# Denominators copied one key tile sooner, their reciprocal behind the first unit's statistics, and the next pair's scales ahead of the last unit's

## The chip, the core and the metric

The kernel runs on one core of a Trainium2 chip. The metric is device time in microseconds (us), the median of several executions; lower is better. Beside the executions that were timed there is one that the hardware profiler recorded.

## What is computed

Two layers over x of shape (8, 768, 32, 32), in float32; each adds its result to its input.

```python
N = H * W                                              # 1024 tokens, 12 heads of 64
x_flat = swapaxes(gn(x).reshape(B, C, N), 1, 2)
q, k, v = split(x_flat @ W_qkv.T)                      # q is not used further
var_v, var_k = var(v, ddof=1), var(k, ddof=1)          # over the 64 channels of a head
scores = var_v @ swapaxes(var_k) * hd ** -0.5          # an outer product, N x N for each head
out = softmax(scores) @ v
x = x + from_tokens(out @ W_proj.T + b_proj)           # layer 0
# layer 1: each channel group of gn(x) is shifted by a whole offset, masked and
# smoothed with a 3 x 3 kernel made of the offset's rest
x = x + displace(gn(x), offset)
```

gn normalises over groups of 24 channels. The scores of a head have rank one, so one row of exponentials is exp(scale of the key x row of the queries).

## The kernel before

Batches follow each other; in a loop over them, the attention of batch b + 1 (function `span`) runs beside the displacement (layer 1) of batch b. Batch 0 is handled ahead of the loop and has no layer-1 work beside it. Every engine has its own program, in which the order is written out by hand; they meet at semaphores alone.

**A batch.** A phase A makes the first six units of K and V (`kv_unit`: two tiles of 128 tokens for one pair of heads, 72 matmuls, line 1096); four units make a pair. Then come six pairs of heads, p = 0 to 5 (MT = 8 key tiles of 128 each, m = 0 to 7). Behind them the output is projected (`phase_c`, line 1150).

**A pair on TensorE.** Two units of a later pair, the weighting of V by the exponentials for key tiles 0 to 3 (`weigh`, line 1135), the two transposes of `k_transpose` (lines 1105, 1106), two more units, the small matmul of `k_spread` (line 1110), key tiles 4 to 7, and the denominators (line 1117) at the end. In pair 4 only two units are left, the transposes stand behind key tile 1 and the spread behind key tile 3; pair 5 has none of these. TensorE's queue stands at the transposes until VectorE has made `kmx` (line 770).

**On ScalarE.** `exps` makes the two exponentials of a key tile (line 607) into a ring of eight; they need the pair's scales `coef` and the broadcast row `a_sb`. `d_copy` copies the denominators of the pair before out of PSUM (line 614). `middle_tap` belongs to layer 1 (line 631), `v_evict` takes V out of PSUM once the unit's statistics are done (line 591).

**On VectorE.** `add_up` adds the exponentials of tiles 1 to 6 (in pairs 4 and 5: 1 to 4) into a sum for each head (line 805); the second head's sum of tile 1 waits for the denominators of the pair before (semaphore `s_d`). `kv_stats` takes the statistics of a unit out of PSUM (line 754), `variances` makes kmx of them, `k_max` (lines 777 to 780) and `k_scales` (lines 785, 788) the scales of the next pair. `d_reciprocal` (line 809) inverts the denominators, `o_normalise` (line 816) uses them; the rest is layer 1's: `taps_y` and `gn` at m = 3, `taps_x` (lines 859 to 864) at m = 6.

**The denominators' way.** They are copied on ScalarE into `d_sb`, spread over 128 partitions by four small DMAs of SyncE (`dt_sb`, line 407), inverted on VectorE, written to DRAM (line 411), broadcast to `r_t` (line 420) and multiplied in at m = 4. The scales' way goes through SyncE too: `at`, to DRAM (line 392), broadcast to `a_sb` (line 401). SyncE works its queue in order. GpSimd writes layer 1's rows to DRAM and gathers the shifted windows from there (line 498).

In code, the waits that the prediction comes to:

```python
act.wait_ge(s_d, b * NP + p + 1)                  # d_copy: denominators complete
dve.wait_ge(s_dt, (b * NP + p) * 64 + 64)         # d_reciprocal: the four DMAs have landed
pe.wait_ge(s_kmx, b * NP + q + 1)                 # k_transpose
dve.wait_ge(s_kmp, b * NP + q + 1)                # k_scales: the spread matmul is done
```

Of the kernel before, what the change touches and what calls it, by code (L numbers as in the profile page):

```python
# [38 lines left out]
def gn_attention_displace(nc, x, w_qkv, w_proj, b_proj, offset, out):  # L39
# [44 lines left out]
    with ctx:  # L84
# [478 lines left out]
        def _(act):  # L563
# [29 lines left out]
            def exps(b, p, m):  # L593
                for s in (0, 1):
                    h = 2 * p + s
                    i = (p * MT + m) * 2 + s
                    if m == 0:
                        if s == 0:
                            act.wait_ge(s_coef, b * NP + p + 1)
                        act.wait_ge(s_a[h % 4], a_count(b, h))  # L600
                    if i >= RING:

                        pj, mj = divmod((i - RING) // 2, MT)
                        act.wait_ge(s_pv, b * (NT // 2) + (i - RING) // 2 + 1)
                        if mj < MD[pj]:
                            act.wait_ge(s_acc, b * NADD + add_count(pj, s, mj))
                    nc.scalar.activation(ring_of(p, s, m), a_sb[:, h % 4, :], ACT.Exp,  # L607
                                         scale=coef[:, h, m:m + 1]).then_inc(s_exp, 1)

            def d_copy(b, p, later):  # L610
                act.wait_ge(s_d, b * NP + p + 1)
                if later or p:
                    act.wait_ge(s_dt, (b * NP + p) * 64)
                nc.scalar.activation(d_sb[:, :], ps[:, D_BANK, :], ACT.Copy).then_inc(s_dsb, 1)
# [11 lines left out]
            def middle_tap(b, t):  # L626

                act.wait_ge(s_sh, (b * CT + t + 1) * 16)
                if t:
                    act.wait_ge(s_fin, b * CT + t)  # L630
                nc.scalar.activation(t_t, g_t, ACT.Copy, scale=taps[:, t, 1, 1:2]).then_inc(s_tap, 1)
# [7 lines left out]
            def span(b, l1, with_next, beside=None):  # L639
                later = l1 is not None  # L640
                for p in range(NP):
                    nxt = UA + p * UQ
                    for m in range(MT):
                        if not later and p == 0 and m == 3:
                            act.wait_ge(s_pads, 2 * CT * 16)
                        exps(b, p, m)
                        if p and m == (3 if p <= 4 else 2):
                            d_copy(b, p - 1, later)
                        if m == 3:
                            if later:  # L650
                                middle_tap(l1, p)
                            if p <= 4:
                                v_evict(b, nxt)
                                v_evict(b, nxt + 1)
                        if m == 7:
                            if p:
                                o_first(b, p - 1)
                            if 1 <= p <= 4:
                                add_bias(b, p - 1)
                            if p <= 3:  # L660
                                v_evict(b, nxt + 2)
                                v_evict(b, nxt + 3)
                        if with_next and (p, m) in X_LOADS:
                            load_x(b + 1, X_LOADS[p, m])
                        if beside is not None:
                            beside(p, m)
# [59 lines left out]
        def _(dve):  # L726
# [20 lines left out]
            def kv_stats(b, u):  # L747

                q, g = divmod(u, UQ)
                dve.wait_ge(s_kv, b * NU + u + 1)  # L750
                for m in (0, 1):
                    for c in range(4):
                        lo = m * 2 * P + c * HD
                        ins = nc.vector.bn_stats(st[:, 2 * g + m, c, :], ps[:, kv_bank[u % 2], lo:lo + HD])  # L754
                ins.then_inc(s_bn, 1)
# [26 lines left out]
            def k_scales(b, q):  # L782

                dve.wait_ge(s_kmp, b * NP + q + 1)
                nc.vector.tensor_tensor(coef[:, 2 * q:2 * q + 2, :], m2[:, 2:4, :],
                                        ps_km.unsqueeze(2).broadcast_to((P, 2, MT)), ALU.subtract).then_inc(s_cch, 1)
                dve.wait_ge(s_cch, b * NP + q + 1)
                nc.vector.tensor_scalar(coef[:, 2 * q:2 * q + 2, :], coef[:, 2 * q:2 * q + 2, :], var_f8[:, 0:1], 0.0,
                                        ALU.mult, ALU.min).then_inc(s_coef, 1)
# [97 lines left out]
            def span(b, l1, with_next, beside=None):  # L887
                later = l1 is not None
                for p in range(NP):
                    nxt = UA + p * UQ  # L890
                    for m in range(MT):
                        add_up(b, p, m, later)
                        if m == 2:
                            if p:
                                d_reciprocal(b, p - 1)
                            if p <= 4:
                                kv_stats(b, nxt)
                        if m == 3:
                            if p <= 4:
                                kv_stats(b, nxt + 1)  # L900
                                variances(b, p + 1)
                            if p == 4:
                                k_max(b, p + 1, later)
                            if later:
                                taps_y(l1, p, g_t, t_t)
                                if p + 1 < CT:
                                    gn(l1, p + 1, g_t)
                        if m == 4:
                            if p <= 3:
                                k_max(b, p + 1, later)  # L910
                            if p == 4:
                                k_scales(b, p + 1)
                            if p:
                                o_normalise(b, p - 1)
                        if m == 5 and p <= 3:
                            kv_stats(b, nxt + 2)
                        if m == 6:
                            if p <= 3:
                                kv_stats(b, nxt + 3)
                                k_scales(b, p + 1)  # L920
                            if later:
                                taps_x(l1, p, t_t)
                        if m == 7 and p:
                            if p == NP - 1 and with_next:
                                x_stats(b + 1, (0, 1))
                            o_second(b, p - 1)
                        if beside is not None:
                            beside(p, m)
# [331 lines left out]
```

## Time and profile before

| | |
|---|---|
| median of 3 runs | 2263.07 us (2258.71 to 2267.14) |
| the profiled execution's own time | 2257.91 us |
| its span, first to last instruction | 2256.3 us |
| mean granted clock of TensorE | 0.956 of full speed |
| TensorE busy | 2036.6 us, 90% |
| VectorE busy | 1676.5 us, 74% |
| ScalarE busy | 1179.1 us, 52% |
| GpSimd busy | 192.3 us, 9% |

The profiled execution lies 5.2 us under the median; what surrounds its span is 1.6 us. The shares are means over stages: a phase A, the pairs and the group's end have different limits. PE stands for TensorE, PEld for its loads of weights, DVE for VectorE, ACT for ScalarE, POOL for GpSimd and SP for SyncE; a q behind a name marks what its sequencer does, such as issuing a DMA.

### The profile page before, as it was taken

The numbers are of one execution on the slowest core, as the hardware profiler recorded it, in microseconds if no ns is written. First come the engines' busy times: TensorE is split into PE (matmuls) and PEld (weight loads), VectorE is DVE, ScalarE is ACT, GpSimd is POOL, SyncE is SP. The second block draws the span as 40 slices with busy tenths as digits, with TensorE's granted clock in tenths as the row PEclk, the third lists the DMA queues.
The fourth block names the chain that finished last, engine by engine and source line by source line (L and its number), as shares of the span: only waits on it lengthen the run. The fifth ranks groups of instructions, "written<-read, shape, count | busy, mean of one in ns | idle before, by whom it ended". The sixth has DMA issues, their size and how long they took to land.

```text
span 2256.3 us, 36312 instructions
## 1 busy us (share of the span) xinstructions
PE 2036.6 (90%) x13036; PEld 1118.5 (50%) x13036; DVE 1676.5 (74%) x3695; ACT 1179.1 (52%) x1285; POOL 192.3 (9%) x215
## 2 busy tenths in 40 slices
PE   3899999998999999999899989999899999999970
PEld 2665346552655436563375625655265543665330
DVE  7676566986678865887668976698668886688837
ACT  5466525664266742667336752566426674265701
POOL 2000000110001100110000100011000110011001
PEclk7999999999999999999999999999999999999995
DMA  6311302334023521335113350233412342133304
GB/s 241 132 49 58 95 11 95 114 115 131 11 100 118 160 68 39 104 110 173 30 53 118 114 161 11 95 114 120 126 31 84 120 163 57 39 119 118 104 20 168
DMA packets 106989, 219.14 MB, mean 97 GB/s; under 512 B 53024, under 2 KB 53792, under 8 KB 106784
## 3 DMA queue, kind: packets, MB, share of 16 engines
q1 hardware_dynamic: 74816, 100.12, 15.1%
q0 software_dynamic: 25920, 94.38, 11.4%
q10 hardware_dynamic: 6048, 22.02, 2.9%
q8 instruction: 114, 1.87, 0.3%
q14 instruction: 91, 0.75, 0.1%
HBM read 158.28 MB, written 57.80 MB: 96 GB/s over the span
## 4 chain that ended last, share of the span: by engine, by line
PE 37%; DVE 27%; DMA 13%; ACT 10%; issue 8%; SPq 3%; POOL 1%; DVEq 0%; ACTq 0%; POOLq 0%
PE ps L1150 13%; PE ps L1135 12%; DVE bt L805 10%; PE ps L1096 9%; ACT ring L607 8%; DVE st L754 6%; DMA a_sb<-a_rows 3%; DMA dt_sb<-d_sb 3%; PE ps L1117 3%; SPq L407 3%; DMA bt<-r_rows 2%; DMA a_rows<-at 2%; DVE bt L849 2%; DVE bt L846 1%; DVE bst_x L728 1%
## 5 line engine op out<-in xcount | busy, mean ns | idle before, releaser
L607 ACT ACTIVATE ring<-a_sb,coef 128x1024 f32<-128x1024 f32 x768 | 810.7, 1136 | 48.5 <-DMA a_sb<-a_rows 33.1
L1096 PE MATMUL ps<-wkv_hi,h_sp 128*128 128x256 f16 x4608 | 786.8, 276 | 11.8 <-DVE h_sp L745 9.9
L1135 PE MATMUL ps<-ring,xv 128*64 128x512 f32 x3072 | 704.0, 606 | 1.4
L1096 PE MATMUL ps<-wkv_lo,h_sp 128*128 128x256 f16 x2304 | 634.7, 275 | 0.0
L1096 PEld LDWEIGHTS ps<-wkv_hi,h_sp 128*128 128x128 f16 x4608 | 455.5, 99 | 103.4 <-issue 31.8
L805 DVE TENSOR_TENSOR bt<-bt,ring 128x1024 f32<-128x1024 f32 x416 | 487.7, 1212 | 1.4 <-ACT ring L607 1.4
L1135 PEld LDWEIGHTS ps<-ring,xv 128*64 128x64 f32 x3072 | 210.0, 139 | 421.3 <-issue 386.5
L591 ACT ACTIVATE xv<-ps 128x256 f32<-128x256 f32 x192 | 73.5, 383 | 653.2 <-DVE st L754 653.2
L1150 PE MATMUL ps<-xv,wp_hi 128*128 128x512 f16 x1152 | 358.9, 389 | 41.0 <-DVE xv L820 28.3
L754 DVE BATCH_NORM_STATS2 st<-ps 128x6 f32<-128x64 f32 x1536 | 216.5, 209 | 57.8 <-PE ps L1096 56.9
L1096 PEld LDWEIGHTS ps<-wkv_lo,h_sp 128*128 128x128 f16 x2304 | 227.8, 99 | 28.1
L1150 PE MATMUL ps<-xv,wp_lo 128*128 128x512 f16 x576 | 224.5, 390 | 0.0
L1150 PEld LDWEIGHTS ps<-xv,wp_hi 128*128 128x128 f16 x1152 | 115.2, 100 | 205.0 <-issue 46.8
L805 DVE TENSOR_TENSOR bt<-ring 128x1024 f32<-128x1024 f32 x96 | 114.3, 1221 | 99.7 <-ACT ring L607 76.6
L809 DVE RECIPROCAL dt_sb<-dt_sb 128x16 f32<-128x16 f32 x48 | 12.1, 253 | 174.4 <-DMA dt_sb<-d_sb 174.4
L624 ACT ACTIVATE xv<-bt 128x1024 f16<-128x1024 f32 x48 | 50.6, 1055 | 160.5 <-DVE bt L816 159.2
L949 DVE SCALAR_TENSOR_TENSOR xv<-ps,proj_f,xv 128x512 f32<-128x512 f32 x96 | 71.3, 745 | 68.9 <-PE ps L1150 68.6
L816 DVE TENSOR_TENSOR bt<-ps,bt 128x1024 f32<-128x1024 f32 x48 | 58.2, 1213 | 73.9 <-DMA bt<-r_rows 73.9
L498 POOL DMA_INDIRECT bt<-shift_rows,first_i x42 | 83.4, 1986 | 162.8 <-DMA shift_rows<-bt 117.1
L1150 PEld LDWEIGHTS ps<-xv,wp_lo 128*128 128x128 f16 x576 | 57.6, 100 | 67.5 <-issue 6.0
L1117 PE MATMUL ps<-ring,ones 128*32 128x512 f32 x640 | 85.2, 605 | 0.0
L506 POOL DMA_DIRECT2D shift_rows<-bt x42 | 23.3, 556 | 633.1 <-DVE bt L834 633.1
(122 smaller groups left out, 1341.3 us busy)
## 6 DMA issues: line engine op xcount, KB each, us to landing
a_sb<-a_rows SPq DMA_DIRECT2D x96, 512.0 KB, 4.8
xv<-in_x POOLq DMA_DIRECT2D x48, 512.0 KB, 3.7
bt<-r_rows SPq DMA_DIRECT2D x96, 256.0 KB, 3.9
h_sp<-in_x ACTq DMA_DIRECT2D x42, 512.0 KB, 4.1
shift_rows<-bt POOLq DMA_DIRECT2D x42, 512.0 KB, 2.9
out<-xv POOLq DMA_DIRECT2D x42, 512.0 KB, 2.9
shift_rows<-ring SPq DMA_DIRECT2D x12, 528.0 KB, 14.0
xv<-in_L_conv_W_qkv SPq DMA_DIRECT2D x4, 1152.0 KB, 8.9
```

The costliest lines, as they stand in the source:

```text
L407: sp.dma_start(dt_sb[32 * g:32 * g + 32, :], d_sb[32 * g:32 * g + 1, :]).then_inc(s_dt, 16)
L498: nc.gpsimd.indirect_dma_start(dst, None, shift_rows[t].rearrange("c r -> (c r)").unsqueeze(0), bass.IndirectOffsetOnAxis(first_i[:, t:t + ...
L591: nc.scalar.activation(v_sb[:, q, 2 * g:2 * g + 2, :], src[:, :, 0:P], ACT.Copy, scale=V_DOWN).then_inc(s_vev, 1)
L607: nc.scalar.activation(ring_of(p, s, m), a_sb[:, h % 4, :], ACT.Exp, scale=coef[:, h, m:m + 1]).then_inc(s_exp, 1)
L754: ins = nc.vector.bn_stats(st[:, 2 * g + m, c, :], ps[:, kv_bank[u % 2], lo:lo + HD])
L805: nc.vector.tensor_tensor(acc_of(p, s), one, ring_of(p, s, m), ALU.add).then_inc(s_acc, 1)
L816: nc.vector.tensor_tensor(r2, ps[:, k:k + 2, :], r2, ALU.mult).then_inc(s_on, 1)
L949: nc.vector.scalar_tensor_tensor(cut, ps[:, pj_bank[u % 6], :], proj_f[:, 0:1], cut, ALU.mult, ALU.add).then_inc(s_x1, 1)
L1096: last = nc.tensor.matmul(ps[:, kv_bank[u % 2], half * 2 * P:(half + 1) * 2 * P], h_sp[:, k, hp, m * P:(m + 1) * P], wkv[wpart][:, k, q * ...
L1117: last = nc.tensor.matmul(ps[32 * g:32 * g + 32, D_BANK, :], ones[:, 0:32], tiles[s][:, j * HALF:(j + 1) * HALF], start=start, stop=stop)
L1135: last = nc.tensor.matmul(ps[s * HD:(s + 1) * HD, o_bank[p % 2] + j, :], v_sb[:, p, m, s * HD:(s + 1) * HD], ring_of(p, s, m)[:, j * HALF: ...
L1150: last = nc.tensor.matmul(ps[:, pj_bank[u % 6], :], wp[wpart][:, k, t * P:(t + 1) * P], o_sp[:, k, op, j * HALF:(j + 1) * HALF], start=(k ...
```

## The change

In each pair, `d_copy` stands behind the exponentials of key tile 2 on ScalarE; so far it stood behind those of tile 3 in pairs 1 to 4, and behind tile 2 in pair 5. On VectorE, `d_reciprocal` moves from key tile 2 to key tile 3, and the statistics of the pair's first unit, which stood behind the reciprocal, move there too and stand ahead of it. The sums of tile 3 thereby come ahead of both. In pairs 0 to 3, `k_scales` stands ahead of the statistics of the last unit.

```diff
@@ ScalarE, span
                         exps(b, p, m)
-                        if p and m == (3 if p <= 4 else 2):
+                        if p and m == 2:
                             d_copy(b, p - 1, later)
@@ VectorE, span
                         add_up(b, p, m, later)
-                        if m == 2:
+                        if m == 3:
+                            if p <= 4:
+                                kv_stats(b, nxt)
                             if p:
                                 d_reciprocal(b, p - 1)
-                            if p <= 4:
-                                kv_stats(b, nxt)
-                        if m == 3:
                             if p <= 4:
                                 kv_stats(b, nxt + 1)
                                 variances(b, p + 1)
...
                         if m == 6:
                             if p <= 3:
+                                k_scales(b, p + 1)
                                 kv_stats(b, nxt + 3)
-                                k_scales(b, p + 1)
                             if later:
                                 taps_x(l1, p, t_t)
```

## Rows read from the trace of the kernel before

**Rows 1.** The page's first part: busy time, share of the span, instructions.
```profile
PE 2036.6 (90%) x13036; PEld 1118.5 (50%) x13036; DVE 1676.5 (74%) x3695; ACT 1179.1 (52%) x1285; POOL 192.3 (9%) x215
```

**Rows 2.** Totals of waits: who waited for whom, us, times, the longest.
```profile
DVE dt_sb L809 <- DMA dt_sb<-d_sb: 174.4, 48, 10.0
...
PE ps L1105 <- DVE kmx L770: 58.7, 30, 4.2
...
ACT ring L607 <- DMA a_sb<-a_rows: 33.1, 18, 3.7
```

**Rows 3.** Busy time by stretch: pairs 1 to 4 of batch 0; batches 1 to 7 summed.
```profile
128.52:252.47 123.95, 123.95 (x859) 69.89 (x860) 88.19 (x235) 80.05 (x89) 0.00 (x0) 1.00 0.24 70
...
sum 921.39, PE 882.48 PEld 491.63 DVE 785.44 ACT 623.59 POOL 114.01; mean PE 126.07 PEld 70.23 DVE 112.21 ACT 89.08 POOL 16.29
```

**Rows 4.** The same view, batch 4: pairs 1, 2, 4, and behind a wait.
```profile
core 0: us, PE busy (x) PEld busy (x) DVE busy (x) ACT busy (x) POOL busy (x), PEclk, DMA share, GB/s
...
1192.43:1224.77 32.34, 32.34 (x230) 19.20 (x230) 27.14 (x63) 20.84 (x24) 3.83 (x3) 1.00 0.35 116
1224.77:1257.84 33.07, 32.41 (x230) 19.19 (x230) 29.46 (x65) 21.96 (x25) 4.37 (x4) 1.00 0.35 113
...
1290.88:1323.54 32.66, 28.51 (x175) 12.53 (x176) 26.22 (x47) 24.67 (x26) 4.04 (x5) 0.95 0.55 170
...
1306.50:1308.00 1.50, 1.42 (x4) 0.39 (x6) 0.72 (x5) 1.25 (x2) 0.00 (x0) 0.50 0.88 208
```

**Rows 5.** TensorE in time: start, length, [idle before, released by]; batch 0, then 4.
```profile
237.34 3.65 PE L1135 MATMUL ps<-ring,xv 128*64 128x512 f32 x16
...
1173.46 0.38 PE L1105 MATMUL ps<-ident,av 128*16 128x128 f32 x1 [2.98 <-DVE kmx L770]
...
1240.42 0.28 PE L1105 MATMUL ps<-ident,av 128*16 128x128 f32 x1 [0.66 <-DVE kmx L770]
...
1306.58 0.38 PE L1105 MATMUL ps<-ident,av 128*16 128x128 f32 x1 [4.15 <-DVE kmx L770]
...
1307.11 4.96 PE L1135 MATMUL ps<-ring,xv 128*64 128x512 f32 x16
```

**Rows 6.** VectorE in time, pair 4 of batch 4.
```profile
1292.89 2.35 DVE L805 TENSOR_TENSOR bt<-ring 128x1024 f32<-128x1024 f32 x2
1295.16 2.35 DVE L805 TENSOR_TENSOR bt<-bt,ring 128x1024 f32<-128x1024 f32 x2
1300.90 0.25 DVE L809 RECIPROCAL dt_sb<-dt_sb 128x16 f32<-128x16 f32 x1 [3.39 <-DMA dt_sb<-d_sb]
...
1304.33 1.14 DVE L754 BATCH_NORM_STATS2 st<-ps 128x6 f32<-128x64 f32 x8
...
1306.37 0.16 DVE L770 TENSOR_REDUCE kmx<-m 128x2 f32<-128x16 f32 x1
```

**Rows 7.** ScalarE in time, pairs 4 and 5 of batch 4.
```profile
1288.34 8.43 ACT L607 ACTIVATE ring<-a_sb,coef 128x1024 f32<-128x1024 f32 x8 [0.18 <-issue]
1296.67 0.57 ACT L614 ACTIVATE d_sb<-ps 128x512 f32<-128x512 f32 x1
...
1324.19 2.18 ACT L607 ACTIVATE ring<-a_sb,coef 128x1024 f32<-128x1024 f32 x2
...
1326.27 1.14 ACT L631 ACTIVATE bt<-bt,taps 128x1024 f32<-128x1024 f32 x1
```

**Rows 8.** VectorE in time, pair 5 and the end of batch 4.
```profile
1329.67 0.25 DVE L809 RECIPROCAL dt_sb<-dt_sb 128x16 f32<-128x16 f32 x1 [2.48 <-DMA dt_sb<-d_sb]
...
1354.45 0.25 DVE L809 RECIPROCAL dt_sb<-dt_sb 128x16 f32<-128x16 f32 x1 [4.58 <-DMA dt_sb<-d_sb]
...
1365.77 1.22 DVE L816 TENSOR_TENSOR bt<-ps,bt 128x1024 f32<-128x1024 f32 x1 [8.02 <-DMA bt<-r_rows]
```

**Rows 9.** VectorE in time, pair 0 of batch 4, its first sums.
```profile
1163.33 2.36 DVE L805 TENSOR_TENSOR bt<-ring 128x1024 f32<-128x1024 f32 x2 [7.31 <-ACT ring L607]
```

**Rows 10.** GpSimd in time, pair 4 of batch 4: the gather of the last windows.
```profile
1319.33 1.85 POOL L498 DMA_INDIRECT bt<-shift_rows,first_i  x1 [6.52 <-DVE xv L864]
```

## The prediction

> **What bounds the kernel now.** I read the page first: TensorE is busy 2036.6 us of a span of 2256.3, twenty points ahead of VectorE's 1676.5 [rows 1], so a change is worth what it takes from TensorE's idle time and from the time that its matmuls run slowly. The totals of waits come next. TensorE's largest wait by name is that of its transpose (line 1105) for VectorE's maxima kmx: 58.7 us in 30 waits. VectorE's largest is that of the reciprocal (line 809) for the denominators' DMA: 174.4 us, all 48 times [rows 2]. Are they one chain? In pair 4 of batch 4 VectorE's order answers: two tiles of sums (each tile is two additions), 3.39 us of waiting for the DMA, reciprocal, then the statistics and sums on which kmx hangs, kmx finished at 1306.53, and 0.05 us later TensorE goes on, after 4.15 us [rows 5, 6]. So the DMA's lateness is passed on to TensorE.
>
> What a pair costs without such a wait is in the trace: batch 0 has no layer-1 work on VectorE, its transposes never wait, and TensorE is busy for all 123.95 us from the end of pair 0's denominators to the end of pair 4's. The same stretch in batches 1 to 7 takes 921.39 us together, TensorE 882.48 of them busy, with as many matmuls [rows 3]. The excess over 7 x 123.95 = 867.65 is 53.74 us: 921.39 - 882.48 = 38.9 idle, and 14.8 in which the same matmuls took longer. The second part is the clock. In pair 4, behind the 4.15 us wait, the granted clock is 0.50 of full speed (the lower of the two levels, 1.2 GHz), and 16 matmuls take 4.96 us that in batch 0 took 3.65 [rows 4, 5]. Behind the wait of 0.66 in pair 2 it stays at 1.00 [rows 4, 5]. By pairs in batch 4: pair 1 takes 32.34 and has nothing to lose, pair 2 takes 33.07 (0.7 too much, and pair 3 repeats it), pair 4 32.66 where 26.92 do (that is 123.95 less three times 32.34) [rows 3, 4], 5.74 too much.
>
> **The change, part by part.** It adds and removes no instruction; three are moved. I count from S, the end of the denominators' matmuls of the pair before: 1290.88 for pair 4 of batch 4 [rows 4].
>
> *The copy.* Eight exponentials take 8.43 us, and the copy (0.57) stands behind them at 1296.67 [rows 7]. Behind six it starts 8.43 x 2/8 = 2.1 us sooner, at 1294.6. What it reads is complete at S, so it needn't wait here. SyncE is idle until then, and the four small DMAs behind it start 2.1 sooner too. From the copy's end (1297.24) to the reciprocal (1300.90) is 3.66 us [rows 6, 7], so the data are there at 1298.8. Queued behind the copy are the exponentials of tile 3, 0.5 later: ready at 1297.3, when VectorE is still at tile 2's sums (until 1297.51) [rows 6]. Hidden, and ScalarE is busy 21.96 of 33.07 us in pair 2 [rows 4].
>
> *The reciprocal and the first statistics behind tile 3's sums.* VectorE's new order in pair 4: sums until 1297.5, tile 3's sums 2.27 more (as from 1292.89 to 1295.16) to 1299.8, first statistics 1.1 to 1300.9, reciprocal 0.2 to 1301.1 with its data there since 1298.8, second statistics and the small chain 2.2 (1304.33 to 1306.53) to 1303.3 [rows 6]. TensorE wants kmx at 1306.58 - 4.15 = 1302.43, S + 11.55. So with nothing else moved the wait falls from 4.15 to 0.9.
>
> *The same with the pairs before it gaining too.* VectorE starts pair 4's sums 2.0 us behind S [rows 6] because the pair before stalled it 3.3 as well; its work in pair 2 is 29.46 us where TensorE's pair is 32.34 at best [rows 4], so without the stalls it catches up within a pair or two. Then the sums begin at S + 0.2 at best (one of them waits for those denominators), end at S + 5.9 with tile 3's, and the first statistics end at S + 7.0. The copy, if ScalarE has run ahead, waits for S, and its data land at S + 0.7 + 3.66 = 4.4: no stall. The second statistics can't start before TensorE's second unit ends: S + 7.9 (1302.43 less 3.65 for the two key tiles between, 1298.8), and kmx is there at S + 10.2. Pairs 1 to 3 want it at S + 15.0 (1240.42 - 0.66 - 1224.77), pair 4 at S + 11.55 [rows 4, 5]. All four waits go, and with pair 4's its slow matmuls. I take the full 53.7; the other bound, 0.9 kept in each pair 4 and the clock up, is 53.7 - 6.3 = 47.4. For pair 5 and the end of the group I take nothing: the copy there was behind tile 2 already, and the reciprocal has its data only at 1329.67, after a wait of 2.48 [rows 8], into which tile 3's sums (2.27) now fall. That chain hangs on the pair's denominators, which shift as a whole.
>
> *Pair 0* keeps its wait. No reciprocal is in it; VectorE sits idle 7.31 us until the exponentials come and then works without a break to kmx, in either order [rows 9]. So some 2.98 us of waiting stay in a batch, with the slow clock behind them (that transpose took 0.38 where pair 2's took 0.28) [rows 5].
>
> *The scales ahead of the last statistics.* The coefficients come by one set of statistics sooner (1.14 long [rows 6]), the last unit's statistics later by two operations on 16 columns, some tenths of a us, and with them ScalarE's copy of V and the next exponentials. TensorE wants the first of these at S + 7.9 = 1298.8; they begin at 1288.34 [rows 7]. With ten us between, the price is nothing. If VectorE has run ahead it now waits for TensorE's spread matmul, which comes directly after that unit: another few tenths, inside its 2.9 of slack.
>
> *What is late next.* The projection and pair 5 follow TensorE. Pair 5's exponentials of tile 3 come 2.5 us ahead of need now (1326.37 [rows 7] against three key tiles behind the pair's start, 1323.54 + 3 x 1.8 = 1328.9 [rows 4, 5]). Walk ScalarE's queue through the new pair 4: tile 4's exponentials start at S + 9.6, when TensorE has freed the ring; four tiles, 8.4, S + 18.0; then it waits for VectorE's normalisation (kmx at 10.2, the answer from TensorE at some 12, layer 1's three operations 3.8, tile 4's sums 2.3, scales 0.4, normalisation 1.2: S + 20.4), two operations of 1.1, S + 22.6; six exponentials, the copy and two more, 9.0, S + 31.6. TensorE wants them at S + 26.9 + 5.4 = 32.3: a margin of 0.7. Thin, but on this side.
>
> The sum: 2257.91 - 53.7 = 2204.2 for an execution like the profiled one. The median of before is 2263.07, 5.2 above that one; the forecast for a median is 2263.07 - 53.7 = 2209.4, and I say 2210.
>
> **Rivals.**
> *Part of pair 4's wait stays* (VectorE doesn't catch up, pair 5 is held a little by ScalarE, or the clock falls by chance at another place). 0.9 kept in seven batches is 2216; with the slow matmuls too, which cost 5.74 - 4.15 = 1.6 in batch 4, 6.3 + 11 = 17 us, 2227. For it: the thin margin in pair 5. Against: VectorE's 2.9 us of slack.
> *GpSimd's gathers.* In pair 4 the gather of the windows stood 6.52 us until VectorE's operation at line 864 ended [rows 10]. A VectorE without idle gaps leaves fewer openings. The middle tap of pair 5, which stands ahead of tile 4's exponentials, waits for that gather (1319.33 to 1326.27, 6.94 us at most [rows 7, 10]). A gather that is pushed behind two more VectorE operations costs some 2 us in pair 5: 7 x 2 = 14, 2223. The Trainium skill speaks for this one (page "SBUF — State Buffer", section "Who interferes with whom"): VectorE with two SBUF inputs and a GpSimd instruction that reads SBUF exclude each other for whole instructions. [...]
> *No change:* exponentials too late. Everything up to kmx now hangs behind tile 3's exponentials and the copy. Were they as late as in pair 0, kmx would still be late. The loads of a_sb make them wait 33.1 us in all, 18 times [rows 2], mostly in pairs 0 and 1; it would have to be every pair. 2255 to 2263.
> *Slower:* the reciprocals' way back. In pairs 1 to 3 the normalisation stands in VectorE's queue at about S + 16.7 (kmx 10.2, layer 1's operations 3.8, tile 4's sums 2.3, the maxima 0.4), and the reciprocal ends at S + 7.1. Where VectorE waited for this way at the end of batch 4 it took 11.07 us (1354.70 to 1365.77, amid other loads) [rows 8]. Over 9.6 VectorE waits; over 9.6 + 2.9 of slack + 1.3 in pair 4 TensorE does. At 17.5 us it would lose some 3.7 in each of three pairs, 11 for the 7.7 gained: 2263 + 7 x 3.4 = 2287. It decides from about 16.5 us, half as long again as that.
>
> **How the numbers follow.** Full gain 0.66 (2200 to 2217: the runs of before spread by 4 either side, and the clock may fall in more or fewer of the seven pairs 0); part of pair 4's wait 0.14 and the gathers 0.12 (2215 to 2236); no change 0.04; slower 0.04. A difference under 0.5%, 11 us, is about what a measurement of this kernel can't tell from none. Faster 0.92, within 0.04, slower 0.04. Range 2198 to 2236: it leaves out the last two cases and the ends of the others.
>
> **What would show it.** Right: in pairs 1 to 4 no wait at line 1105, pair periods of 32.3 and pair 4 at 26.9, the clock at 1.00 through pair 4; VectorE's wait at line 809 gone in pairs 1 to 4, its idle time now at the first sums and before the second statistics; total wait at line 1105 about 20 us, all of pair 0. Wrong: waits of TensorE at line 1135 in pair 5, a wait at line 816 in pairs 1 to 4, or a pair 4 still at half clock.

## The result and the profile after

The changed kernel takes 2205.32 us (median of four runs, 2201.63 to 2210.82), the kernel before, on the same chip, 2261.9 (2258.71 to 2267.14). The ratio is 0.975, with a 95% interval of 0.9717 to 0.9782: faster by 2.5%, and 5 us below the forecast of 2210. The profiled execution has a time of 2210.82 and a span of 2209.2, the longest of its four, where the profiled one of before was the shortest of its own; so the two spans differ by 47.1 us and the medians by 56.6. Of the page, the engines' busy time first:

```profile
PE 2025.0 (92%) x13036; PEld 1118.1 (51%) x13036; DVE 1681.8 (76%) x3695; ACT 1183.2 (54%) x1285; POOL 190.5 (9%) x215
```

Against [rows 1] TensorE is busy 11.6 us less with the same 13,036 matmuls, because fewer of them run at the lower granted clock. Next the totals of waits of the changed kernel (who waited for whom, us, times, the longest). TensorE's transposes are one line higher now, at 1104.

```profile
DVE bt L816 <- DMA bt<-r_rows: 90.4, 16, 8.0
DVE bt L805 <- ACT ring L607: 85.4, 29, 7.7
...
DVE dt_sb L809 <- DMA dt_sb<-d_sb: 45.0, 21, 9.4
...
ACT ring L607 <- DMA a_sb<-a_rows: 40.0, 27, 3.8
...
DVE bt L805 <- PE ps L1116: 35.8, 26, 2.4
...
PE ps L1104 <- DVE kmx L770: 19.9, 7, 3.0
```

The wait for kmx has fallen from 58.7 us in 30 waits [rows 2] to 19.9 in seven, one for each pair 0; the reciprocal's from 174.4 in 48 to 45.0 in 21, those of pair 5 and of the groups' ends, and short ones of 0.3 to 1.0 in pair 1. Next the busy time by stretch: first pairs 1 to 4 together, of batches 1, 4 and 7, with the sum over batches 1 to 7; then pairs 1, 4 and 5 of batch 4 one by one.

```profile
core 0: us, PE busy (x) PEld busy (x) DVE busy (x) ACT busy (x) POOL busy (x), PEclk, DMA share, GB/s
388.93:512.87 123.94, 123.94 (x858) 69.96 (x860) 113.37 (x237) 88.77 (x97) 15.81 (x16) 1.00 0.40 131
...
1172.85:1296.80 123.95, 123.95 (x858) 69.92 (x860) 111.65 (x237) 86.72 (x95) 16.46 (x16) 1.00 0.38 127
...
1950.94:2074.88 123.94, 123.94 (x858) 69.92 (x860) 113.36 (x237) 88.60 (x96) 15.93 (x16) 1.00 0.36 123
sum 867.61, PE 867.61 PEld 489.52 DVE 788.12 ACT 614.16 POOL 111.66; mean PE 123.94 PEld 69.93 DVE 112.59 ACT 87.74 POOL 15.95
```

```profile
1172.85:1205.19 32.34, 32.34 (x229) 19.23 (x230) 30.26 (x65) 24.32 (x27) 4.38 (x4) 1.00 0.40 131
...
1269.87:1296.80 26.93, 26.93 (x175) 12.23 (x176) 21.97 (x44) 18.40 (x20) 3.31 (x4) 1.00 0.45 147
1296.80:1320.97 24.17, 23.79 (x120) 6.99 (x120) 19.23 (x20) 16.03 (x16) 1.07 (x2) 1.00 0.54 177
```

TensorE is now busy for the whole of each stretch, at a clock of 1.00: 867.6 us against the 921.39 of [rows 3], 53.8 less. VectorE does the same work (788.12 us, before 785.44 [rows 3]). The last row has something new, pair 5 at 24.17 us with a gap of 0.4 in it. Pair 4 of batch 4 in time, where S is 1269.87; TensorE first (with the transpose of pair 0), then VectorE, then ScalarE:

```profile
1153.75 0.28 PE L1104 MATMUL ps<-ident,av 128*16 128x128 f32 x1 [2.98 <-DVE kmx L770]
...
1281.36 0.28 PE L1104 MATMUL ps<-ident,av 128*16 128x128 f32 x1
1281.67 3.65 PE L1134 MATMUL ps<-ring,xv 128*64 128x512 f32 x16
...
1302.47 1.94 PE L1134 MATMUL ps<-ring,xv 128*64 128x512 f32 x8 [0.37 <-ACT ring L607]
```

```profile
1270.03 1.23 DVE L805 TENSOR_TENSOR bt<-ring 128x1024 f32<-128x1024 f32 x1 [1.46 <-PE ps L1116]
1271.17 4.62 DVE L805 TENSOR_TENSOR bt<-bt,ring 128x1024 f32<-128x1024 f32 x4
1275.71 1.15 DVE L754 BATCH_NORM_STATS2 st<-ps 128x6 f32<-128x64 f32 x8
1276.77 0.24 DVE L809 RECIPROCAL dt_sb<-dt_sb 128x16 f32<-128x16 f32 x1
1277.88 1.15 DVE L754 BATCH_NORM_STATS2 st<-ps 128x6 f32<-128x64 f32 x8 [0.87 <-PE ps L1095]
...
1279.93 0.16 DVE L770 TENSOR_REDUCE kmx<-m 128x2 f32<-128x16 f32 x1
```

```profile
1270.02 0.60 ACT L614 ACTIVATE d_sb<-ps 128x512 f32<-128x512 f32 x1 [0.68 <-PE ps L1116]
...
1292.85 1.15 ACT L607 ACTIVATE ring<-a_sb,coef 128x1024 f32<-128x1024 f32 x1 [0.73 <-DMA a_sb<-a_rows]
1294.55 1.15 ACT L607 ACTIVATE ring<-a_sb,coef 128x1024 f32<-128x1024 f32 x1 [0.55 <-DMA a_sb<-a_rows]
```

The transpose waited 4.15 us at this place and the 16 matmuls behind it took 4.96 [rows 5]; now it doesn't wait and they take 3.65. VectorE waits for TensorE twice (1.46 and 0.87 us), which means that it has caught up; the reciprocal finds its data there.

To see what each change moved I compare stages. A stage runs from one end of the denominators' matmuls of a pair to another, in the profiled execution; "between" is from pair 5's end to the end of the next pair 0, seven times (us).

| kernel | median | ratio [95%] | pairs 1-4, batches 1-7 | pair 5, all 8 | between |
|---|---|---|---|---|---|
| before | 2261.9 | | 921.4 | 188.6 | 783.5 |
| after | 2205.32 | 0.975 [0.9717, 0.9782] | 867.6 | 190.3 | 786.1 |
| copy alone | 2234.88 | 0.9882 [0.9839, 0.9924] | 897.9 | 188.6 | 782.7 |
| order alone | 2206.11 | 0.9739 [0.9695, 0.9783] | 867.6 | 189.9 | 784.6 |
| scales alone | 2265.19 | 1.0015 [0.9995, 1.0034] | 925.1 | 188.6 | 784.7 |
| later transposes | 2252.77 | 0.9962 [0.9941, 0.9984] | 911.5 | 196.1 | 780.2 |
| after, again | 2207.45 | 0.9762 [0.9735, 0.9789] | 867.6 | 191.2 | 789.0 |
| after + pair 0 | 2179.98 | 0.9645 [0.9617, 0.9673] | 867.6 | 191.4 | 757.5 |
| copy later | 2292.17 | 1.0145 [1.0109, 1.018] | 957.4 | 188.6 | 780.6 |
| copy behind tile 1 | 2204.59 | 0.9727 [0.971, 0.9745] | 868.3 | 189.1 | 784.5 |
| copy alone, small x load | 2201.39 | 0.9713 [0.9684, 0.9741] | 867.6 | 188.6 | 781.4 |
| before, small x load | 2252.42 | 0.9935 [0.9915, 0.9955] | 917.8 | 188.6 | 780.0 |
| pair 0 + x loads | 2181.76 | 0.9637 [0.9613, 0.9661] | 867.6 | 188.6 | 764.5 |
| pair 0, order only | 2180.62 | 0.9631 [0.9607, 0.9655] | 867.6 | 190.3 | 758.9 |

In the table, "small x load" stands for kernels in which a load of x is cut down, "order" for VectorE's order and "x loads" for ScalarE's loads of x, all explained below. Each ratio is to runs of the kernel before on the same chip (medians 2260.45 to 2265.73). The first two columns of stages are steady; "between" differs by some us from one execution to the next for kernels that have the same code there, and makes up most of the spread of the times.

### The profile page after: what moved, and what is told of

Same layout as the page of the kernel before. It is cut to its first block, busy times and chain, and to the rows that moved or that the text cites. A ratio compares the mean times of both kernels' runs of the same rounds, so it can differ in the third digit from the quotient of the medians.

```text
span 2209.2 us, 36312 instructions
## 1 busy us (share of the span) xinstructions
PE 2025.0 (92%) x13036; PEld 1118.1 (51%) x13036; DVE 1681.8 (76%) x3695; ACT 1183.2 (54%) x1285; POOL 190.5 (9%) x215
## 3 DMA queue, kind: packets, MB, share of 16 engines
q0 software_dynamic: 25920, 94.38, 11.5%
## 4 chain that ended last, share of the span: by engine, by line
PE 75%; DMA 10%; DVE 9%; issue 3%; ACT 2%; SPq 1%; POOL 1%; ACTq 0%; DVEq 0%; POOLq 0%
PE ps L1095 29%; PE ps L1134 26%; PE ps L1149 13%; PE ps L1116 5%; DMA a_sb<-a_rows 3%; DMA bt<-r_rows 2%; DVE st L754 1%; DMA a_rows<-at 1%; ACT ring L607 1%; DVE bst_x L728 1%; DMA dt_sb<-d_sb 1%; DVE bt L805 1%; DMA cs_rows_y<-mv_y 1%; DMA xv<-in_L_conv_W_qkv 1%; SPq L407 1%
## 5 line engine op out<-in xcount | busy, mean ns | idle before, releaser
L1134 PE MATMUL ps<-ring,xv 128*64 128x512 f32 x3072 | 693.3, 597 | 2.3 <-ACT ring L607 0.6
L816 DVE TENSOR_TENSOR bt<-ps,bt 128x1024 f32<-128x1024 f32 x48 | 58.3, 1214 | 90.4 <-DMA bt<-r_rows 90.4
L575 ACT ACTIVATE ring<-h_sp,rb_x 128x1024 f32<-128x1024 f32 x42 | 51.0, 1229 | 41.1 <-DMA rb_x<-gs_rows_x 41.1
```

The source lines that it names most:

```text
L575: nc.scalar.activation(y_t[t], x_in[:, t, :], ACT.Identity, bias=rb["x"][:, t, 1:2], scale=rb["x"][:, t, 0:1]).then_inc(s_hf, 1)
L816: nc.vector.tensor_tensor(r2, ps[:, k:k + 2, :], r2, ALU.mult).then_inc(s_on, 1)
L1134: last = nc.tensor.matmul(ps[s * HD:(s + 1) * HD, o_bank[p % 2] + j, :], v_sb[:, p, m, s * HD:(s + 1) * HD], ring_of(p, s, m)[:, j * HALF: ...
```

## The experiments

**Which part of the change does it?** Three kernels, each with one of its parts.

Copy alone:
```diff
-                        if p and m == (3 if p <= 4 else 2):
+                        if p and m == 2:
                             d_copy(b, p - 1, later)
```


> Only the copy moves (behind the exponentials of key tile 2); VectorE keeps the old order. Theory A, each of the two moves is enough once the pairs have caught up: the copy starts at S (waits for the denominators), its data land at S + 4.4, the reciprocal waits some 0.8 us behind tile 2's sums, first statistics, tile 3's sums and second statistics follow, kmx at about S + 10.3, ahead of S + 11.55. Pair periods 32.34 and 26.92 as in the changed kernel, excess over 7 x 123.95 under 3 us, time about 2208 to 2212. Theory B, the moves add up: the copy brings its 2.1 us and no more; no wait in pairs 1 to 3, 2.0 us left at the transposes of pair 4, 7 x 2.0 = 14 us of excess without and about 25 with a slow clock, time 2220 to 2235.

Order of VectorE alone:
```diff
-                        if m == 2:
-                            if p:
-                                d_reciprocal(b, p - 1)
+                        if m == 3:
                             if p <= 4:
                                 kv_stats(b, nxt)
-                        if m == 3:
+                            if p:
+                                d_reciprocal(b, p - 1)
                             if p <= 4:
```


> Only the reciprocal and the first unit's statistics move on VectorE; the copy stays behind tile 3 and the scales behind the last statistics. Theory A: tile 3's sums and the first statistics (2.3 + 1.1 us) fill the 3.3 us of waiting, so VectorE catches up and the copy then comes at about S + 1.8; kmx at S + 10.3 in the steady state, no wait in any of pairs 1 to 4, excess under 3 us, time 2208 to 2212. Theory B: without the sooner copy the data are late also for the new place, some 0.9 us stay in pair 4 and the clock may fall: 2214 to 2230. Theory C, the sooner copy is the whole of it: nothing gained, 2255 to 2265.

Scales alone:
```diff
                             if p <= 3:
-                                kv_stats(b, nxt + 3)
                                 k_scales(b, p + 1)
+                                kv_stats(b, nxt + 3)
```


> Only the scales move ahead of the last unit's statistics, in the kernel before. All theories of the prediction: nothing on TensorE's path, the waits at the transposes as before (58.7 us in all within 2), excess over 7 x 123.95 of 52 to 56 us, time within 0.3% of before. If the last statistics were on the path (through the copy of V and the exponentials), some 0.4 us in each of four pairs, 28 times: 11 us slower.

Measured: order alone 2206.11, which is the whole gain: 867.6 us for the seven stretches, no wait at a transpose but in pair 0. Scales alone 2265.19, which can't be told from no change. Copy alone 2234.88: the theory that either edit is enough by itself fell, and the one that they add up had the time right (at the very end of its range) but the wait in pair 4 too small, 2.0 us where 2.4 to 3.4 were left. Pairs 1 to 3 take 32.34 in this kernel, so they have nothing more to give, and yet VectorE doesn't get ahead. The reason shows in pair 4 of batch 4 of the kernel with the copy alone, S = 1275.50. In time: VectorE, ScalarE, SyncE's queue and GpSimd, then TensorE; below them GpSimd's load of x and the first and the third of the four small DMAs (KB each, us from issue to landing).

```profile
1277.03 2.36 DVE L805 TENSOR_TENSOR bt<-ring 128x1024 f32<-128x1024 f32 x2
1279.30 2.36 DVE L805 TENSOR_TENSOR bt<-bt,ring 128x1024 f32<-128x1024 f32 x2
1284.38 0.25 DVE L809 RECIPROCAL dt_sb<-dt_sb 128x16 f32<-128x16 f32 x1 [2.72 <-DMA dt_sb<-d_sb]
...
1278.73 0.57 ACT L614 ACTIVATE d_sb<-ps 128x512 f32<-128x512 f32 x1
...
1279.33 2.46 SPq L407 DMA_DIRECT2D dt_sb<-d_sb  x4
...
1280.42 0.54 POOL L516 DMA_DIRECT2D xv<-in_x  x1 [3.12 <-DMA out<-xv]
...
1290.08 0.38 PE L1105 MATMUL ps<-ident,av 128*16 128x128 f32 x1 [3.02 <-DVE kmx L770]
```

```profile
xv<-in_x POOLq DMA_DIRECT2D x1, 512.0 KB, 3.6
dt_sb<-d_sb SPq DMA_DIRECT2D x1, 2.0 KB, 1.7
...
dt_sb<-d_sb SPq DMA_DIRECT2D x1, 2.0 KB, 3.5
```

The copy ends at 1279.30 and the reciprocal's data come 5.08 us later, where it was 3.66 before [rows 6, 7]. GpSimd's load of the next batch's x, 512 KB, is issued at 1280.42, among the four small DMAs, and lands 3.6 later, at 1284.0; the reciprocal goes on 0.36 behind that. The first two small DMAs were issued ahead of the load and landed 1.7 us after their issue, at 1281.0 and 1281.7; the other two were issued behind it and landed right behind it, at 1284.04 and 1284.36. (All four count up one semaphore; these are the times at which each quarter of its count was reached.) So my assumption of 3.66 us was wrong for this place. And the lateness renews itself: reciprocals of pairs 2, 3 and 4 come at 1219.36, 1251.91 and 1284.38, 32.5 apart, a little more than TensorE's 32.34, so VectorE doesn't catch up from pair to pair. How one pair's lateness makes the next pair's copy late I only infer: the copy waits in ScalarE's queue behind exponentials, and these behind work that waits for VectorE. In pairs 1 to 3 the transposes have 3.45 us more room and hardly wait (0.12 us at most); pair 4's have not.

**Is it the load?** The copy alone with the load cut from 1024 to 64 columns of each tile, so that most of x is missing from the result, and the same cut in the kernel before.
```diff
-                        pool.dma_start(x1[:, t - 1, :], x_t[b + 1, :, t - 1, :]).then_inc(s_x1in[t - 1], 16)
+                        pool.dma_start(x1[:, t - 1, 0:64], x_t[b + 1, :, t - 1, 0:64]).then_inc(s_x1in[t - 1], 16)
```


> copy_only, and GpSimd's load of the next batch's x1 brings 64 of the 1024 columns of each tile instead of all (the rest of the residual is left out of the result). Theory L: with the load out of the way the four DMAs land 3.0 to 3.6 us behind the copy, VectorE catches up, pair 4's wait goes: excess over 7 x 123.95 near 0, 2205 to 2212. Theory Q: nothing changes against copy_only, 2232 to 2238.

> The control of copy_small_load: the kernel before with the same small load (the same part of the result left out). Before, the last of the four DMAs landed 1.0 to 1.1 us behind the load, 3.6 behind the copy, so the load held it little if at all: the excess stays at 45 to 54 us and the time at 2255 to 2265. Should it fall by itself to 2210, the load, and not the copy's place, would be what the change is about.

Measured: 2201.39 and 2252.42. Pair 4 of batch 4 of the copy alone with the small load, VectorE, ScalarE and GpSimd, then the same view of DMAs as above:

```profile
1269.11 0.25 DVE L809 RECIPROCAL dt_sb<-dt_sb 128x16 f32<-128x16 f32 x1 [0.70 <-DMA dt_sb<-d_sb]
...
1264.90 0.60 ACT L614 ACTIVATE d_sb<-ps 128x512 f32<-128x512 f32 x1 [0.49 <-PE ps L1117]
...
1266.62 0.54 POOL L516 DMA_DIRECT2D xv<-in_x  x1 [3.74 <-DMA out<-xv]
```

```profile
xv<-in_x POOLq DMA_DIRECT2D x1, 32.0 KB, 2.1
```

The data now come 3.61 us behind the copy's end, pair 4's wait is gone in all seven batches (867.6 us), and the copy alone is as fast as the whole change. In the kernel before the same cut leaves pair 4's wait at 3.9 to 4.2: the reciprocal starts 3.6 us behind the copy with either load (3.61 with the small one and 3.66 with the full one in pair 4 of batch 4), so there the load was not what held it. Both times lie 3 to 4 us under the ranges expected, and why stays open. Where the load is large, the completion of small DMAs issued behind it follows the load's. The Trainium skill has the rule for it (page "DMA: Bandwidth & Descriptors", section "Queues, rings and completion order"): the semaphore's increment is a write that lands only behind every earlier write of that DMA engine, across its queues. The trace agrees, 5.08 us with the load of 512 KB and 3.61 with 32 KB; whether it is this rule, or the small DMAs only share the engines with the load, was not tried apart.

**Does the copy's place set it in both directions?** The copy of the kernel before moved behind the middle tap, 1.05 us later, and moved one tile further ahead than the change does.
```diff
-                        if p and m == (3 if p <= 4 else 2):
+                        if p == 5 and m == 2:
                             d_copy(b, p - 1, later)
...
                                 middle_tap(l1, p)
+                            if p and p <= 4:
+                                d_copy(b, p - 1, later)
```


> The dose the other way: the kernel before with the copy of pairs 1 to 4 one operation later, behind layer 1's middle tap (1.05 us). If the DMA's landing sets kmx, as I hold, each of these pairs waits 1.05 us longer at the transposes (pair 1: from some 0.2 to 1.2, pairs 2 and 3: 0.7 to 1.7, pair 4: 4.15 to 5.2), 7 x 4.2 = 29 us slower, and the waits at line 1105 rise from 58.7 to about 88; time about 2291. If VectorE's own work sets it: no difference.

```diff
-                        if p and m == (3 if p <= 4 else 2):
+                        if p and m == (1 if p <= 4 else 2):
                             d_copy(b, p - 1, later)
```


> As copy_only, but the copy of pairs 1 to 4 stands one key tile sooner still, behind tile 1; VectorE keeps the old order. In copy_only the copy ended 2.1 us sooner and yet the last of its four small DMAs landed only 0.3 us behind the landing of GpSimd's 512 KB load of x1 (1284.36 against 1284.03 in pair 4 of batch 4), 5.1 us behind the copy instead of 3.6. Theory L (the small DMAs queue behind that load): another 2.1 us on ScalarE bring nothing or little, unless the copy comes so early that its DMAs land ahead of the load; pair 4 keeps 2 to 3 us of waiting, time 2225 to 2235; where they do get ahead of it, 2208 to 2215. Theory Q (ScalarE's queue sets the loop reciprocal, statistics, exponentials, copy): the loop gets 2.1 us shorter, the wait of pair 4 goes, 2208 to 2212 in every case.

Measured: copy later 2292.17, with pair 4's transpose waiting as far beyond 4.15 as the copy was moved. TensorE in pair 4 of batch 4 of the kernel with the later copy:

```profile
1322.28 0.38 PE L1107 MATMUL ps<-ident,av 128*16 128x128 f32 x1 [5.20 <-DVE kmx L772]
```

The four pairs of the seven batches take 36.0 us longer together, 1.29 for each of 28, where 29 us were expected. So before the change 1.05 us at the copy cost a pair at least as much. In the other direction, copy behind tile 1: 2204.59. Its small DMAs get ahead of the load in some pairs and land just behind it in others (in pair 4 of batch 4 the reciprocal still waits, 1.91 us, until 1268.24), but 2.1 us sooner is enough: transposes wait 0.23 and 0.30 in two of the seven pairs 4, and nowhere else but pair 0. This run doesn't decide between the two theories of its expectation, since both allowed such a gain; the small load does, for it removed the waits with ScalarE's queue in the order of the copy alone.

**Is it enough that TensorE asks later?** The kernel before with the transposes of pair 4 two key tiles later.
```diff
-                        if p <= 4 and m == (3 if p <= 3 else 1):
+                        if p <= 4 and m == 3:
                             k_transpose(b, p + 1)
-                        if m == 3 and p == 4:
+                        if m == 5 and p == 4:
                             k_spread(b, p + 1)
```


> The kernel before with pair 4's two transposes two key tiles later on TensorE (behind tile 3 instead of tile 1) and the spread matmul behind tile 5; VectorE and ScalarE unchanged, so kmx stays late (S + 15.6). If pair 4's loss is the wait and the clock behind it: TensorE works 3.65 us of the 4.15 away, 0.5 stays, the clock stays at full speed, pair 4 at about 27.5 instead of 32.7 to 34: a gain of 7 x (5.5 to 6) = 36 to 40 us, 2222 to 2227; pairs 2 and 3 keep their 0.7. If the clock falls all the same: 10 less, about 2235. If the scales that now come later were on the path (the next pair's exponentials late): pair 5 longer, and less than half of the gain.

Measured: 2252.77, and I had expected 2222 to 2227; of the three cases, the one with pair 5 longer and less than half of the gain came. TensorE in pair 4 of batch 4 of this kernel, then ScalarE:

```profile
1298.95 0.28 PE L1105 MATMUL ps<-ident,av 128*16 128x128 f32 x1 [0.70 <-DVE kmx L770]
...
1301.61 5.35 PE L1135 MATMUL ps<-ring,xv 128*64 128x512 f32 x16 [2.28 <-ACT ring L607]
```

```profile
1297.87 0.38 ACT L591 ACTIVATE xv<-ps 128x256 f32<-128x256 f32 x1 [2.93 <-DVE st L754]
...
1299.37 8.42 ACT L607 ACTIVATE ring<-a_sb,coef 128x1024 f32<-128x1024 f32 x8 [1.12 <-issue]
```

The transpose's wait fell to 0.70, but one that had stood behind it appears: ScalarE's copy of V waits for the second statistics, which are as late as before, the next exponentials stand behind it in ScalarE's queue, and TensorE waits 2.28 for them (2.2 to 2.4 in six of the seven batches, 1.0 in the last) and runs slowly after. The spread comes later too, and pair 5 takes 24.5 instead of 23.57. VectorE's lateness had two takers, and this edit removed one.

**What do pair 0's waits cost?** The changed kernel, and in pair 0 the two sets of statistics and the small chain ahead of tile 1's sums.
```diff
                     for m in range(MT):
+                        if m == 1 and p == 0:
+                            kv_stats(b, nxt)
+                            kv_stats(b, nxt + 1)
+                            variances(b, p + 1)
                         add_up(b, p, m, later)
                         if m == 3:
-                            if p <= 4:
+                            if 1 <= p <= 4:
                                 kv_stats(b, nxt)
...
-                            if p <= 4:
+                            if 1 <= p <= 4:
                                 kv_stats(b, nxt + 1)
```


> The changed kernel once more, as the control of this call: 0.975 of before within 0.003; pairs 1 to 4 without a wait, excess over 7 x 123.95 near 0, pair 0's wait of 2.98 in each batch, and in some batches pair 5 up to 0.6 us over 23.58.

> The changed kernel, and in pair 0 both units' statistics and the chain to kmx stand ahead of the first sums on VectorE, in the 7.3 us in which it was idle. Theory A, pair 0's wait is VectorE's order: kmx at about 1165 instead of 1173 in batch 4, TensorE's transposes there never wait, and the clock doesn't fall behind them: 2.98 and up to some 3 us in each of seven batches, 20 to 30 us, 2176 to 2186. Theory B, the wait is the exponentials' lateness, which stays: the sums start 1.5 us later, the scales of pair 2 come no sooner, and pair 1 or 2 now waits: 2195 to 2205.

Measured: 2207.45 and 2179.98. VectorE, then TensorE, in pair 0 of batch 4 of the kernel with the edit:

```profile
1127.44 1.15 DVE L754 BATCH_NORM_STATS2 st<-ps 128x6 f32<-128x64 f32 x8 [2.81 <-PE ps L1099]
1131.37 1.15 DVE L754 BATCH_NORM_STATS2 st<-ps 128x6 f32<-128x64 f32 x8 [2.78 <-PE ps L1099]
...
1133.43 0.16 DVE L770 TENSOR_REDUCE kmx<-m 128x2 f32<-128x16 f32 x1
...
1139.42 0.28 PE L1108 MATMUL ps<-ident,av 128*16 128x128 f32 x1
```

kmx is there 5.8 us before TensorE asks, because the statistics fill the time in which VectorE sat idle for 7.31 us [rows 9]. "Between" falls by 28.7 us, from 786.1 to 757.5: 19.9 are the seven waits, and 8.7 is what the 64 matmuls of line 1095 behind them took beyond the 7.15 us that they take elsewhere, added over the seven batches. The second run of the changed kernel fits as well: "between" is 789.0, 31.5 more than with the edit, and it has 20.1 us of waits with 10.4 of slow matmuls behind them.

**What is the new gap in pair 5?** The kernel above, with the loads of x one by one.
```diff
-            X_LOADS = {(4, 3): (0, 1), (5, 0): (2,), (5, 1): (3,), (5, 4): (4,), (5, 5): (5,)}
+            X_LOADS = {(5, 0): (0,), (5, 1): (1,), (5, 2): (2,), (5, 3): (3,), (5, 4): (4,), (5, 5): (5,)}
```


> The kernel pair0 (statistics ahead of the sums in pair 0), and ScalarE issues the next batch's loads of x behind key tiles 0 to 5 of pair 5, one each, instead of two behind tile 3 of pair 4 and the rest in pair 5. If pair 5's extra 0.4 to 1.5 us come from the loads of a_sb (heads 10 and 11) landing late beside those two loads, pair 5 takes 23.57 in each batch and ScalarE waits for a_sb there no more: 2 to 3 us less than pair0 (191.38 to 188.6 for the eight pairs 5), 2176 to 2179 where pair0 has 2180; the time alone can't tell that, the trace can. If the later loads hold the statistics of x at the group's end: slower by up to 10 us.

And the kernel above with copy and scales back at their old places, to see whether these two edits are needed when nothing else waits.

> The kernel pair0 with the copy back behind tile 3 and the scales back behind the last statistics: of the change only VectorE's order is kept. order_only says that the order alone is the whole gain: no wait in pairs 1 to 4, 2180 within 4 us, as pair0. If the copy matters once pair 0 no longer waits (pair 1 then starts with VectorE further behind), pair 1 or 2 waits some tenths: 2183 to 2190.

Measured: 2181.76 and 2180.62, neither apart from 2179.98. The x loads do remove pair 5's wait: 188.6 us instead of 191.4, with 23.57 in every batch, and ScalarE's total wait for a_sb falls from 31.0 to 26.5. But the 2.8 us can't be told in the time, and "between" is 7.0 us longer in this profile (764.5), 4.4 of them in TensorE's wait for VectorE's operation at line 820 at the group's end, 37.1 for 32.7. The expectation had named that price, later loads that hold the group's end; whether it is one, or the spread of "between", a single profile can't tell. Copy and scales add nothing here either.

## Why the prediction was right, by its steps

- *The readings.* TensorE's busy share is 16 points ahead of VectorE's (90% and 74%), not twenty. In the walk of ScalarE's queue the terms named add up to S + 19.7, not 20.4; measured, the normalisation of pair 4 ends at S + 20.1.
- *The excess of 53.74 us in pairs 1 to 4, taken in full.* Measured 53.8. Every pair has the period named, 32.34 and 26.92, at a granted clock of 1.00.
- *The walk from S.* First statistics predicted to end at S + 7.0, measured 1276.86 - 1269.87 = 7.0; kmx S + 10.2, measured 10.2; the transpose asks at S + 11.5, as said. VectorE did catch up, and its sums wait 1.46 us for the denominators. The reciprocal's wait is gone in pairs 2 to 4; in pair 1 0.3 to 1.0 us are left, which nothing hangs on.
- *The copy's term.* Here the working was right in sum and wrong in its parts. I gave the copy 2.1 us and the order the rest. By the runs the order alone has the whole gain, since it takes the wait for the DMA off the path to the first statistics and lets tile 3's sums cover it; the copy alone has some 28 us, about half. The 3.66 us from copy to data is not a constant: it is 4.9 to 5.4 in pairs 2 to 4 of the copy alone, where GpSimd's x load falls among the small DMAs. In the changed kernel the data of pair 4 of batch 4 landed at S + 5.2, not at S + 4.4. With the order changed it doesn't matter, because the reciprocal has until S + 7.0.
- *Scales.* Priced at nothing, measured 1.0015 [0.9995, 1.0034].
- *Pair 5.* A margin of 0.7 us was predicted. What came is a pair 5 that takes up to 0.6 us longer in batches 2 to 5, 1.7 us in all. The walk left out that ScalarE, now earlier, meets the loads of a_sb (0.73 and 0.55) beside the loads of x; with these one by one pair 5 loses nothing (188.6). This part is shown by the run. So one of the signs named for being wrong did come, TensorE's waits at the weighting in pair 5 (now line 1134): 0.37 us in batch 4 and 0.21 in batch 5, too small to move the time.
- *Pair 0.* Its waits stayed, 2.98 us in six batches and 2.04 in the last, as predicted, with slow matmuls behind them in six of the seven batches, 8.7 us in all (before: in five, 8.6).
- *The rest.* In the profiled executions +1.7 in pair 5, +2.7 between, +1.9 in batch 0 and +0.4 at the end stand against the 53.8; apart from pair 5's I found no cause, and runs of one kernel differ by as much there. The largest wait in "between", TensorE's for VectorE's line 820 at the group's end, is 28.3 us before and 33.0 after. It is 24.4 to 32.2 in all profiles with VectorE's old order and 32.0 to 37.1 in those with the new one, so the order may cost something there; that is not shown.
- *The size.* For an execution like the profiled one 2204.2 was forecast and 2210.82 measured; for the median 2209.4, and 2205.32 measured. The sum took nothing outside the pairs, and both misses are within what the executions of one kernel differ by: that the median came within 5 us is in part luck, that the pairs gave 53.8 is not.

**The rivals.** Part of pair 4's wait stays: it doesn't in the changed kernel, but it is what the copy alone does. GpSimd's gathers: the prediction read the wait of [rows 10] as one for VectorE's line 864, and that reading was wrong. GpSimd in pairs 3 and 4 of batch 4 of the kernel before, and the two writes of `shift_rows` (KB, us from issue to landing):

```profile
1277.75 0.54 POOL L506 DMA_DIRECT2D shift_rows<-bt  x1 [13.98 <-DVE bt L834]
1281.46 2.76 POOL L498 DMA_INDIRECT bt<-shift_rows,first_i  x1 [3.17 <-DMA shift_rows<-bt]
...
1312.26 0.54 POOL L506 DMA_DIRECT2D shift_rows<-bt  x1 [15.45 <-DVE bt L834]
```

```profile
shift_rows<-bt POOLq DMA_DIRECT2D x1, 512.0 KB, 2.9
...
shift_rows<-bt POOLq DMA_DIRECT2D x1, 512.0 KB, 6.3
```

The gather starts 0.8 us after this write has landed, in pair 3 (1277.75 + 2.9) as in pair 4 (1312.26 + 6.3, and 1319.33), and 41 of the 42 gathers of the kernel before start 0.8 to 0.9 us after theirs. Line 864 only happens to end just then, and the program has no wait for it there. What goes with VectorE's operations is how long GpSimd works on the gather: 2.74 to 2.77 us where two sums of line 805 ran from its start, 1.01 to 1.07 where only statistics and scales did. In the changed kernel the wait is 6.71 us in batch 4, with the write landing after 6.4, and the middle tap behind the gather does not wait there; in batch 5 it waits 1.13 us, for a gather that lands 9.5 us after its start, and in the second run of that kernel three times, 3.6 us in all. So something of this rival came, in pair 5's few tenths of a us, and not by line 864.

No change: it would have needed exponentials as late as in pair 0. The reciprocals' way back: the total at line 816 rose from 73.9 to 90.4, but all 16 waits are in pair 5 and at the groups' ends; in pair 2 of batch 4 the normalisation starts at 1221.89, S + 16.7, just as walked, with no wait.

## What to carry to other kernels

When an engine waits for a small transfer, first see what stands behind the wait in its queue: moving other ready work ahead of the wait took the whole gain here, and starting the transfer sooner took half of it. If removing one wait gives less than its length, look for a second taker of the same lateness, as with the later transposes, and for lateness that comes back in each round with a period as long as the bound's, as with the copy alone: it isn't worked off, though every engine has idle time. An engine that is idle at the start of a group, waiting for one input, is the place for work whose other input is already there: pair 0's statistics gave half as much again as the change did.

## What the runs showed of the hardware

**Small transfers behind a large one.** Four DMAs of 2 KB on SyncE's queue, issued around a 512 KB load of GpSimd's, let the reciprocal go on 5.08 us after the copy, 0.36 behind the large load's landing; around a load of 32 KB, 3.61. The two issued ahead of the large load landed 1.7 us after their issue, the two behind it 3.5 and 3.2.

**The clock behind a wait.** In the traces of before, after, after again, copy alone, order alone, later copy and later transposes, transposes outside pair 4 that waited 0.6 to 1.8 us were always followed by 64 matmuls at full speed, 7.15 us; those that waited 1.9 to 3.3 took 8.3 to 9.9 in most cases and 7.15 in the others, with nothing in the length of the wait to tell them apart. Every wait of about 4 us in pair 4 of the kernel before was followed by slow ones, 4.8 to 6.4 us for what takes 3.65; in pair 4 of the copy alone two waits of 3.39 were followed by full speed, and one of 2.40 by 4.9 us. So in these traces a wait's cost is its length and up to some 2.8 us more. Behind pair 0's in batch 4 of the changed kernel, three stretches of 2 us, the granted clock in the last column but two:

```profile
1153.70:1155.70 2.00, 1.95 (x13) 1.47 (x14) 1.97 (x2) 2.00 (x3) 0.00 (x0) 0.71 0.00 0
1155.70:1157.70 2.00, 2.00 (x11) 1.39 (x10) 1.97 (x3) 2.00 (x3) 0.00 (x0) 0.50 0.00 0
1157.70:1159.70 2.00, 2.00 (x20) 1.75 (x18) 2.00 (x3) 2.00 (x3) 0.56 (x1) 0.94 0.28 113
```
